# A gated cross-attention block: one kind of unit and the next batch's x in other slots, and the closing products rearranged

## The reference, cut to what matters

```python
x = x + tanh(g_xattn) * xattn(layernorm(x), ctx)      # 4 batches of 256 rows, 512 wide; ctx 1601 rows
x = x + tanh(g_ffn) * ffn(layernorm(x))

# xattn: 32 query heads of 128, in groups of 4 that share one of 8 key/value heads
q = query @ Wq + bq
k, v = split(kv @ Wkv + bkv)
attn = softmax(q k^T / sqrt(128))
return (attn @ v) @ Wo + bo

# ffn: base product and 8 low-rank experts of rank 16, of which the top 2 per row count
base = x @ base_W.T
probs = softmax(x @ router_W.T); top 2, weights divided by their sum
mid = (x @ lora_A) * weight of its expert
return base + 2 * (mid @ lora_B)
```

## Time and profile before

| | before |
|---|---|
| median of 3 runs | 2308.6 us (2307.56 to 2309.07) |
| profiled execution | 2309.07 us, span 2307.1 us |
| PE busy | 2257.9 us of the span |
| DVE busy | 1812.2 us |
| ACT busy | 1667.0 us |
| POOL busy | 1631.9 us |
| granted PE clock, mean | 0.999 |

### The profile page before, as it was taken

The page is one execution under the profiler, slowest core; times in us unless marked ns, Lnnn a source line. Parts: engine busy times, 40 slices in busy tenths (PEclk is TensorE's granted clock), DMA queues, the critical chain, the costliest instruction groups (busy, mean ns, idle before and its releaser), DMA issues.

```text
span 2307.1 us, 37400 instructions
## 1 busy us (share of the span) xinstructions
PE 2257.9 (98%) x12361; PEld 1940.2 (84%) x12361; DVE 1812.2 (79%) x3162; ACT 1667.0 (72%) x3156; POOL 1631.9 (71%) x1372
## 2 busy tenths in 40 slices
PE   7999999999999999999999999999999999999988
PEld 6888888887888888888888888888888888888865
DVE  5888888888787787787778787787788778787785
ACT  4777777776777777777777777777777777777763
POOL 5887886976668678757657778776756756766762
PEclk9999999999999999999999999999999999999999
DMA  7344353564233342325214333333422213222211
GB/s 259 129 158 137 118 162 110 173 202 150 88 113 110 100 159 95 128 87 202 92 49 137 111 128 120 111 130 112 160 83 96 92 60 111 67 98 88 68 66 55
DMA packets 137567, 271.85 MB, mean 118 GB/s; under 512 B 21664, under 2 KB 54944, under 8 KB 137120
## 3 DMA queue, kind: packets, MB, share of 16 engines
q1 hardware_dynamic: 122400, 255.71, 32.7%
q10 hardware_dynamic: 14976, 13.74, 2.6%
HBM read 202.44 MB, written 66.97 MB: 117 GB/s over the span
## 4 chain that ended last, share of the span: by engine, by line
PE 80%; DVE 9%; POOL 4%; issue 3%; ACT 3%; DMA 0%; ACTq 0%; SPq 0%; POOLq 0%; DVEq 0%
PE psW L419 12%; PE psW L420 12%; PE psW L421 12%; PE psS L419 7%; PE psS L421 7%; PE psS L420 7%; PE psW L616 7%; PE psW L617 6%; PE psW L618 6%; PE psW L475 3%; DVE psum_ L1309 3%; DVE mrun L1274 2%; POOL xs L805 2%; PE psW L483 1%; DVE pl L1053 1%
## 5 line engine op out<-in xcount | busy, mean ns | idle before, releaser
L805 POOL TENSOR_TENSOR xs<-xs,mb 128x512 f32<-128x512 f32 (+1 forms) x832 | 1067.8, 1309 | 475.6 <-ACT mb L876 475.6
L1274 DVE TENSOR_TENSOR mrun<-psS,mrun 128x512 f32<-128x512 f32 (+1 forms) x704 | 482.4, 685 | 339.5 <-ACT xs L876 338.3
L876 ACT ACTIVATE xs<-psS 128x512 f32<-128x512 f32 (+1 forms) x832 | 496.2, 597 | 242.6 <-PE psS L421 230.9
L1053 DVE TENSOR_TENSOR pl<-psP,ph 128x512 fp32r<-128x512 f32 (+1 forms) x672 | 459.2, 683 | 81.7 <-ACT ph L998 76.9
L998 ACT ACTIVATE ph<-xs 128x512 fp32r<-128x512 f32 (+1 forms) x832 | 518.9, 624 | 0.2 <-PE psW L618 0.2
L1309 DVE TENSOR_TENSOR psum_<-psP,psum_ 128x512 f32<-128x512 f32 (+1 forms) x672 | 456.9, 680 | 0.9 <-POOL pl L809 0.8
L995 ACT ACTIVATE psP<-xs 128x512 f32<-128x512 f32 (+1 forms) x672 | 401.2, 597 | 34.5 <-DVE rinv L1216 13.1
L419 PE MATMUL psS<-ql,kh 128*128 128x512 f32 (+1 forms) x832 | 339.4, 408 | 6.8 <-DVE mrun L1274 5.7
L616 PE MATMUL psW<-ph,vh 128*128 128x512 f32 (+1 forms) x832 | 333.9, 401 | 6.0 <-POOL pl L809 4.2
L618 PE MATMUL psW<-ph,vl 128*128 128x512 f32 (+1 forms) x832 | 328.2, 394 | 0.0
L420 PE MATMUL psS<-qh,kh 128*128 128x512 f32 (+1 forms) x832 | 328.0, 394 | 0.0
(11 more groups left out here) (188 smaller groups left out, 4377.6 us busy)
## 6 DMA issues: line engine op xcount, KB each, us to landing
wqh<-scr_wq SPq DMA_DIRECT2D x96, 256.0 KB, 2.7
wql<-scr_wq SPq DMA_DIRECT2D x96, 256.0 KB, 3.0
woh<-scr_wo SPq DMA_DIRECT2D x48, 512.0 KB, 3.3
wol<-scr_wo SPq DMA_DIRECT2D x48, 512.0 KB, 4.2
rbc<-scr_r ACTq DMA_DIRECT2D x52, 256.0 KB, 3.4
scr_wq<-wqh SPq DMA_DIRECT2D x32, 256.0 KB, 2.1
scr_wq<-wql SPq DMA_DIRECT2D x32, 256.0 KB, 2.6
scr_wo<-woh SPq DMA_DIRECT2D x16, 512.0 KB, 2.6
```

The source lines that it names most:

```text
L805: eng.tensor_tensor(tile, tile, mb[0:rows_of(t), U % 2, :], ALU.subtract).then_inc(s_sub)
L876: return eng.activation(hi, src, ACT.Copy)
L1053: return eng.tensor_tensor(lo, src, f32(hi), ALU.subtract)
L1274: eng.tensor_tensor(run, psS[0:rows, s % 2, :], a, ALU.max).then_inc(s_m)
```

## The change

Four things are done.

- In the third-kind units `p0` goes from slot 4 to slot 7 (ahead of `r` where there is one), `p1` from 7 to 8, `q0` from 8 to 9, `q1` from 10 to 11. `x0` and `x1` leave them. They go to slots 1 and 2 of the units with U % 16 = 15, whose `q0` and `q1` go to slots 7 and 8. `divide` goes from slot 8 to slot 9 in the units that follow the string `TURN` and in those with `r`, and POOL's cuts of query weights in batch 0's third-kind units one slot later.
- Behind the last score, base products are issued one at a time (`ya` to `yd`), the last unit's `b` stands one slot earlier, six gates are turned in two banks (four and two together) after slot 8, and DVE computes the router's weights in slots 835 and 836 instead of 831 and 832.
- The last unit's P·V is not divided. ACT and DVE split it as it is, the output projection is made for each of the two heads apart, and DVE multiplies each with `rtg` (`rinv` times the gate) as it adds it. The value bias goes through the projection by itself (job `c`, six matmuls), and job `r` of the last unit is gone.
- POOL's order for the last unit: the three `pl` come before the merge.

```diff
-        return 9 if sum_by_mem(V) else 8
+        return 9 if MEM_LO <= V < MEM_SUM else 8 if V < UN - 2 else 10 if V == UN - 2 else 6
...
-        "m,v11 - b,v12 k2 p0 s k3 r,p1 q0 - q1 x0 o0,x1",
+        "m,v11 - b,v12 k2 - s k3 p0,r p1 q0 - q1 o0",
...
+    NEXT_X = "m x0 b,x1 k0 p1 s k1 q0 q1 k2 - o0 o1"
...
-        names_of = {0: "k1 - k2 v0 q0 k3 q1 v1 - v2 - v3 -", UN: "- - - - - s - r - - o0 - o1",
-                    UN + 1: "- - - - - s - r - - o0 o1",
+        names_of = {0: "k1 - k2 v0 q0 k3 q1 v1 - v2 - v3 -", UN: "- - - - - - - - s r - - o0",
+                    UN + 1: "- p1 - - s c o0 o1",
...
-                     -8: "mi4", -7: "mi5 rt0", -1: "m", 0: "b o ya0", 1: "yb0 ga0 ga1", 2: "yl0 ga2 ga3",
-                     3: "ya1 ga4 ga5", 4: "yb1", 6: "yl1", 8: "ya2", 9: "yb2", 11: "yl2",
-                     14: "ya3", 16: "yb3", 17: "yl3", 21: "ya4"}.items():
+                     -8: "mi4", -7: "mi5 rt0", -1: "m ya0 b", 0: "o yb0", 1: "yc0", 2: "yd0", 3: "ya1", 4: "yb1", 5: "yc1", 6: "yd1", 8: "ga0",
+                     9: "ga4", 11: "yl0 yl1", 14: "ya2", 15: "yb2"}.items():
...
-            cuts[at + (9 if u == 2 else 7)] += halves("q", 2 * U + 4)
-            cuts[at + (11 if u == 2 else 9 if u % 2 else 8)] += halves("q", 2 * U + 5)
+            cuts[at + (10 if u == 2 else 7)] += halves("q", 2 * U + 4)
+            cuts[at + (12 if u == 2 else 9 if u % 2 else 8)] += halves("q", 2 * U + 5)
...
+            def proj_o_apart(t):
+
+                have_weight("o", UN - 1, NU)
+                pe.wait_ge(s_ol, UN)
+                for h in range(2):
+                    if t:
+                        take(("o", UN - 1, 2 + h))
+                    cs = slice(h * 256 + t * 128, h * 256 + (t + 1) * 128)
+                    three(apart(t, h), oh[:, cs], ol[:, cs], woh[:, h, :], wol[:, h, :]).then_inc(s_o)
...
-            for name in "yb4 yl4 ya5 yb5 yl5 ht6 ht7 mi6 mi7 ya6 yb6 ya7 ga6 ga7 yb7 yl6 yl7".split():
+            for name in ("yc2 yd2 yl2 ya3 yb3 yc3 yd3 ht6 ht7 yl3 mi6 mi7 ya4 yb4 yc4 yd4 yl4 ya5 yb5 yc5 yd5 yl5 ya6 yb6 yc6 yd6 "
+                         "ga6 ga7 ya7 yb7 yl6 yc7 yd7 yl7").split():
...
-                "S0,S1 S2,S3 S4,S5 M,L0 S6,L1 S7,L2 A2,S8 S9 S10 S11 S12 - -")]
+                "S0,S1 S2,S3 S4,L0 L1,L2 M,S5 S6,A2 S7 S8 S9 S10 S11 S12 -")]
...
-                if s == TN:
-                    route_weights(1)
...
-                if s == TN - 1:
+                if s == TN + 3:
                     route_second(1)
+                if s == TN + 4:
+                    route_weights(1)
...
+            for t in range(2):
+                for h in range(2):
+                    dve.wait_ge(s_o, 2 * UN - 2 + 2 * t + h + 1)
+                    dve.wait_ge(s_acd, 2 * UN - 1 + t if h == 0 else 2 * UN + 2 * t + 1)
+                    eng.scalar_tensor_tensor(acc[:, t, :], apart(t, h), rtg[:, 2 * h + t:2 * h + t + 1], acc[:, t, :],
+                                             ALU.mult, ALU.add).then_inc(s_acd)
```

More of the change, by code:

```diff
@@ L219, in gated_block @@
         rinv = sb("rinv", [128, 2, 4], F32)
+        rtg = sb("rtg", [128, 4], F32)
+        bvh = sb("bvh", [128, 1], F32R)
+        bvl = sb("bvl", [128, 1], F32R)
         steps = sb("steps", [128, 40], F32)
@@ L348, in bank_of, with apart, gated_together @@
             return psW[:, bank[key], :]
+        def apart(t, h):
+            return bank_of(("o", UN - 1, 2 + h)) if t else psP[:, h, :]
         def gates_of(i):
-            return f32(cst[:, 128 * (i - 2):128 * (i - 1)]) if 2 <= i < 6 else midT[:, i % 2, :]
+            return f32(cst[:, 128 * i:128 * (i + 1)]) if i < 4 else midT[:, i % 2, :]
+        def gated_together(i):
+            return {0: 4, 4: 2, 6: 1, 7: 1}[i]
         def y_bank(i):
@@ L509, in ffn_gate @@
             def ffn_gate(i):
-                pe.wait_ge(s_wt, i + 1)
+                n, no = gated_together(i), (0, 4, 6, 7).index(i) + 1
+                pe.wait_ge(s_wt, i + n)
                 o = take(("ga", i, 0))
-                eng.transpose(o[:, 0:128], mid[:, i, 0:128], ident[:, :]).then_inc(s_gt)
-                emptied(("ga", i, 0), s_gc, i + 1)
+                for j in range(n):
+                    m = eng.transpose(o[:, 128 * j:128 * (j + 1)], mid[:, i + j, 0:128], ident[:, :])
+                m.then_inc(s_gt)
+                emptied(("ga", i, 0), s_gc, no)
             def ffn_base(i, k):
@@ L524, in ffn_base @@
                         pe.wait_ge(s_yc, i - 1)
-                for k in (k, k + 1):
-                    eng.matmul(y_bank(i), hT[:, i, k, :], bw_sb[:, k, :], start=k == 0, stop=False)
+                eng.matmul(y_bank(i), hT[:, i, k, :], bw_sb[:, k, :], start=k == 0, stop=False)
             def ffn_lora(i):
-                pe.wait_ge(s_gc, i + 1)
+                pe.wait_ge(s_gc, 1 if i < 4 else 2 if i < 6 else i - 3)
                 eng.matmul(y_bank(i), gates_of(i), lb_sb[:, :], start=False, stop=True).then_inc(s_y)
@@ L540, in job @@
                     proj_q(n, part)
+                elif kind == "o" and n == UN - 1:
+                    proj_o_apart(part)
+                elif kind == "c":
+                    proj_bias()
                 elif kind == "o":
@@ L955, in divided @@
                 u = V % NU
-                act.wait_ge(s_on, V + 1)
+                if V == UN - 1:
+                    act.wait_ge(s_pv, NT * UN)
+                else:
+                    act.wait_ge(s_on, V + 1)
                 if V:
                     act.wait_ge(s_o, 2 * V)
+                if V == UN - 1:
+                    upper(oh[:, :], bank_of(("pv", V, 0))).then_inc(s_oh)
+                    return
                 eng.activation(oh[:, :], bank_of(("pv", V, 0)), ACT.Identity, bias=bkv_sb[:, 8 + u // 2:9 + u // 2]).then_inc(s_oh)
@@ L1021, in _ @@
                         ffn_inner(n)
-                    elif kind == "ga":
-                        ffn_gated(n)
                 if 0 <= V < UN and s % NT == on_slot(V) and not sum_by_mem(V):
                     divided(V)
+                for kind, n, part in jobs.get(s - 2, []):
+                    if kind == "ga":
+                        ffn_gated(n)
                 if s in (0, 2):
@@ L1243, in divide @@
             def divide(V, step):
+                if V == UN - 1:
+                    if step == 0:
+                        dve.wait_ge(s_oh, UN)
+                        lower(ol[:, :], bank_of(("pv", V, 0)), oh[:, :]).then_inc(s_ol)
+                    return
                 if step == 0:
@@ L1259, in goes_first, with goes_later @@
                 return kind == "s" and sum_by_mem(n)
+            def goes_later(kind, n, part):
+                return kind == "yl" or kind == "o" and n == UN - 2
             def running_max(s):
@@ L1293, in _ @@
                 for j in jobs.get(s - 1, []):
[L1294 removed]
+                    if (j[0] not in "ms" or not TN - NT < s <= TN) and not goes_first(*j) and not goes_later(*j):
                         after_job(*j)
[L1296 to L1297 removed]
                 T = s - EXP
@@ L1314, in _ @@
                         eng.tensor_tensor(total, pair_of(UT)[:, 0, :], total, ALU.add).then_inc(s_a)
+                for j in jobs.get(s - 2, []):
+                    if goes_later(*j):
+                        after_job(*j)
                 if TN - NT <= s < TN:
@@ L1327, in _ @@
                     floored_var(2, NQ)
+                if s == 27:
+                    dve.wait_ge(s_bvh, 1)
+                    lower(bvl[:, :], bkv_sb[:, 15:16], bvh[:, :]).then_inc(s_bvl)
                 if s == 26:
```

60 lines of the change are left out of this document (40 added, 20 removed).

## The result

| | before | after |
|---|---|---|
| median, first set | 2308.84 us (4 runs, 2307.56 to 2310.20) | 2323.29 us (4 runs, 2322.58 to 2323.74) |
| median, second set | 2308.44 us (11 runs, 2306.24 to 2311.24) | 2320.58 us (4 runs, 2319.28 to 2321.04) |
| ratio to before | 1 | 1.0062 [1.0049, 1.0074], then 1.0051 [1.0036, 1.0066] |
| span of the profiled execution | 2307.1 us | 2320.6 us, then 2318.2 us |

The change makes the kernel slower, by 14.5 us in the first set and 12.1 us in the second. Forecast were +5.7 us, 2303 to 2319. The direction is right, and both medians lie above the range.

A forecast was written before the change was run, and what follows sets the result against it. PE, busy 2257.9 of 2307.1 us, was taken as the bound. Terms 3.7 + 3.3 + 1.0 + 3.2 - 1.2 - 4.05 = +5.95, taken as +5.7, gave 2308.6 + 5.7 = 2314.3 us, range 2303 to 2319.

The forecast's parts named there:

- The end: Behind the last score: removed waits -6.6, added matmuls +0.95, new waits +1.6, together -4.05 us (range -6 to -2).
- the rival that had the end bound by DVE: At the end, DVE's norms fall behind PE's list and return 2 us: 2316 us; chance 0.05.
- The third-kind units without `r`: Six units, batches 1 to 3: +0.5 at first P·V, +0.9 at last `ql`, -0.74 at slot 12; +3.7 us.
- The units with `r`: `p1` waits 1.6 us for `p0`'s bank instead of 1.0; +3.3 us for units 30 and 46, +1.0 for 62.
- Batch 0: Units 6 and 10: full POOL passes a late `p1` on to the next unit's P·V, 1.6 us each; +3.2 us.
- Unit 14 and x: `x0`'s wait and slow clock go, gaining 4.6 us; with costs, -1.2. Moved x in units 15, 31, 47 costs 0.
- The new waits don't come: Waits at first P·V (0.5) and last `ql` (0.5 to 0.9) stay away, 11 us less: 2303 us; chance 0.2.
- The clock rival: Clock falls after a wait near 3 us, in unit 15 or at the end: 2317 to 2321 us; chance 0.1.

The follow-up runs named there:

- e4: The changed kernel with the second turning of gates moved from slot 9 to slot 13, behind the low-rank products: 2320.07 us, ratio 1.0046.
- e8: e1 with its end reordered (second gate turning in slot 845, low-rank products in 844, some base products later): 2305.00 us, ratio 0.9979.
- e10: The changed kernel with only its end put in the order of e8: 2318.32 us, ratio 1.0041.
- e6: The changed kernel with `p0` back in slot 4 of the third-kind units: 2314.93 us, ratio 1.0024.
- e7: The changed kernel with `q1` in slot 10 instead of 11 of the third-kind units: 2313.53 us, ratio 1.0025.
- e2: The kernel before with only `x0`, `x1` moved to slots 1 and 2 of units 15, 31, 47 and those units' queries to 7 and 8: 2307.50 us.
- e1: The changed kernel with third-kind units, division and POOL's cuts as before, keeping the moved x and the new end: 2307.19 us, ratio 0.9992.
- e5: The changed kernel with batch 0's third-kind units (6, 10, 14), their cuts and division as before; x stays in unit 15: 2316.11 us, ratio 1.0033.
- e11: The changed kernel with `p0` in slot 4 and `q1` in 10 of later third-kind units, batch 0 as in e5, end of e8: 2300.74 us, ratio 0.9967.
- e13: e11 with unit 62 as in the kernel before: 2300.63 us, ratio 0.9955.

## Why the prediction was right or wrong

**The end: the step that failed.** The prediction wrote "New waits: the low-rank product in slot 843 needs gates that ACT copies behind `rbc` and `oh` of unit 62 ... 1.3. Another 0.3 lies before the last projection", and came to -4.05. Measured is -0.3. The old waits did go, at about the forecast price: -6.6 and +0.95, with 2.95, 1.2 and 1.06 us of new losses, make -0.44. What I got wrong is who waits first for the gates' copy. I named a reader of the data, and overlooked that the next turning takes the bank of that copy two slots earlier: 2.95 us, and 1.2 us of half clock in this execution (in five of seven with this wait), for the 1.3. The bias was priced as six matmuls and not as a new first reader of the last weights: 1.06 us for the 0.3. e4, e8 and e10 show it: with the turning later 2.65 us come back, with e8's order, which removes both waits, 3.15 to 3.35 (up to 1.5 us of each is the clock). Without any new wait the forecast's own terms would give -5.65. The stretch of e8 is 3.4 us shorter than before, and of e10 3.2; what is missing is four small waits, three of them on DVE, 1.26 us idle together in e8. So the rival that had the end bound by DVE was right in kind and small.

**The third-kind units without `r`: right.** Places, causes and sum (+4.1 for six, forecast +3.7). e6 and e7 add what the sum could not say: mainly the last `ql` binds; as long as it is late, most of the wait at the P·V is time that would otherwise be lost behind it.

**The units with `r`: right in mechanism.** The wait of `p1` for `p0`'s bank is 1.53 us at all four, and goes with `p0`'s slot (e6). Stretches 30 to 37 and 46 to 53 cost 4.5 instead of 3.3; 1.0 of the difference is x, which I cost at 0 in units 31 and 47 "the cover being slots of 2.8 us next to each bare one" and which costs 0.5 each (e2). Unit 62 with 63 cost 1.65 for 1.0: the forecast named DVE's two norms there and gave them no price, and in slot 11, where unit 22 has no wait, PE is idle for 0.44 and 0.41 us behind DVE.

**Batch 0: right.** 2.8 us for 3.2, POOL's 26.5 us of work unchanged, and the loss gone with e1's string back (e5).

**Unit 14 and x: right in sum, by two errors; that is luck.** x's leaving gives 5.4 us where I had 4.6, but unit 15 pays 2.4 us of it back at once (e2); the third-kind string then costs 2.3 where I had 3.45 for all of it. Over the whole kernel x is the second term that was mis-sized: forecast was a gain of 4.6 us with nothing to pay for it, and from unit 6 to the last score it is 2.6 us in e1 and 2.3 in e2. With the end's 3.75 us and the 1.5 us of units 0 to 5, its 2 us make up nearly all of the 7.55 us between forecast and trace. The fall of the clock was priced in unit 14 alone. The trace before has another one: in unit 0 PE was idle for 3.44 us ahead of 30.62, and the granted clock was 0.50 from 32 to 35 us.

**The rivals.** "The new waits don't come" fell: in batches 1 to 3 all came, at the forecast places. The clock rival, 2317 to 2321, had a wait near 3 us "in unit 15 behind POOL or at the end" with the clock falling behind it, and at the end just this came, 2.95 and 1.2 us of the 7.55; its time is the second set's. It had chance 0.1, and did not say what PE would wait for. In unit 15 no such wait came. And 1.5 us of the profiled difference lie ahead of any changed unit; in its second profile the same kernel reached unit 6 2.4 us sooner, 0.9 ahead of the kernel before.

## What to carry to other kernels

When a step is moved into a gap, look for its first waiter in three lists: who reads its data, who takes its buffer next, and which load its own operands wait for; here the second and third were the error at the end. Where buffers are handed out in turn, write that turn down for the new order ahead of costing anything. Put a short step that frees a bank ahead of long steps on the engine that frees it, and where two engines are level at a unit's edge, remove the one late step that binds (one query half, one slot earlier, took 0.86 us from unit 22) and not the waits that stand ahead of it.

## What the runs showed of the hardware

The granted clock does not follow from the length of a wait. Stretches with the same instructions and nearly the same waits ran at either level. In unit 15, behind idle times of 0.93 and 0.83 us, e2 kept its clock; e5, behind 0.96 and 0.83 us, did not (e1 and e8 were like e2, e11 and e13 like e5):

```profile
547.00:549.00 2.00, 2.00 (x14) 1.71 (x13) 2.00 (x4) 2.00 (x5) 0.64 (x1) 1.00 0.00 0
```

```profile
547.00:549.00 2.00, 2.00 (x6) 1.52 (x5) 2.00 (x4) 1.33 (x4) 1.69 (x2) 0.50 0.00 0
```

That is 14 matmuls in 2 us against 6, and 1.3 us for unit 15. At the start of the kernel, PE idle for 2.65 us ahead of the matmul at 31.10 was followed by 0.68 over 31 to 36 us in the first profile of the changed kernel, while 2.49 us of idle time in the second was followed by 1.00. The data came 1.4 us earlier there too, and unit 0 took 3.1 us less:

```profile
31.00:36.00 5.00, 4.90 (x21) 4.78 (x22) 1.77 (x4) 1.11 (x2) 1.49 (x1) 0.68 0.91 305
```

```profile
31.00:36.00 5.00, 5.00 (x36) 4.74 (x35) 2.79 (x4) 3.51 (x6) 1.34 (x1) 1.00 0.88 297
```

In e4 even the idle time of 1.43 us in unit 63, which the kernels before and after have as well without a loss, was followed by a clock of 0.58 for 4 us, and unit 63 took 1.6 us more; of the fifteen traces, all with this wait, e4, e6 and e11 show the fall. So waits of 0.9 to 3 us had a second price of 1.2 to 1.6 us at these places in some executions and none in others. The runs of one kernel spread with it: of the 25 of the kernel before beside e1 to e4 the fastest (2307.2 us) had a mean granted clock of 0.999 and the slowest (2313.2 us) one of 0.995. What decides in which execution the clock falls, no run here shows. The Trainium skill, in "TensorE: Matmul & The Clock Gate", "HAM oscillation — how this bites in real kernels", says that an engine left waiting between bursts starts the next one throttled; the runs agree that this happens behind waits, and show beside it that it need not.
